# The delta rule of a two-layer sequence kernel: segment states, outputs, norm and gate on the matrix engine in a transposed layout, without a trip through memory

## Time and profile before

| | us |
|---|---|
| median of 3 runs | 1028.77 |
| lowest, highest | 1027.17, 1031.47 |
| the profiled execution | 1028.87 |
| span of its trace, first to last instruction | 1027.1 |

### The profile page before, as it was taken

How to read it: one execution, slowest core, us unless ns; L and a number is a source line. 1 busy time by engine, 2 the same in 40 slices (tenths; PEclk the granted TensorE clock), 3 DMA queues, 4 the chain that set the end, 5 groups by cost and what they waited for, 6 DMA issues and landing times.

```text
span 1027.1 us, 21006 instructions
## 1 busy us (share of the span) xinstructions
PE 652.3 (64%) x8802; PEld 463.8 (45%) x8802; DVE 690.6 (67%) x1280; ACT 383.5 (37%) x894; POOL 252.1 (25%) x179
## 2 busy tenths in 40 slices
PE   3899999999999999999987898930000000000036
PEld 2677776666776677667666364820000000000024
DVE  6377774465666566656536732389999999956987
ACT  2655555423332333233032121574454544420024
POOL 6300001000000000000010002154777777732920
PEclk9999999999999999999797799985555555555556
DMA  4100000000000000000000030000000000020001
GB/s 168 22 8 8 13 13 12 2 2 2 13 2 1 12 2 2 2 2 2 2 2 2 0 84 0 2 1 0 1 0 0 0 0 0 0 36 11 0 0 41
DMA packets 15485, 12.11 MB, mean 12 GB/s; under 512 B 8208, under 2 KB 13072, under 8 KB 15264
## 3 DMA queue, kind: packets, MB, share of 16 engines
q1 hardware_dynamic: 15392, 10.79, 4.3%
HBM read 7.21 MB, written 1.48 MB: 8 GB/s over the span
## 4 chain that ended last, share of the span: by engine, by line
PE 51%; DVE 22%; issue 14%; POOL 7%; ACT 3%; DMA 1%; SPq 1%; DVEq 0%; POOLq 0%; ACTq 0%
PE PS L550 7%; PE PS L526 7%; PE PS L425 4%; POOL arena L1001 4%; PE PS L343 3%; PE PS L331 3%; PE PS L319 3%; PE PS L542 3%; PE PS L512 3%; PE PS L673 2%; POOL arena L1007 2%; DVE arena L1169 2%; DVE arena L606 2%; PE PS L311 2%; PE PS L432 2%
## 5 line engine op out<-in xcount | busy, mean ns | idle before, releaser
L872 PE MATMUL PS<-W,arena 128*64 128x128 f32 x64 | 6.7, 403 | 311.7 <-DVE arena L1191 311.7
L606 DVE TENSOR_TENSOR arena<-PS,C 128x512 f32<-128x512 f32 x160 | 105.6, 686 | 100.8 <-PE PS L526 100.8
L872 PEld LDWEIGHTS PS<-W,arena 128*64 128x64 f32 x64 | 6.5, 226 | 311.9 <-DVE arena L1191 311.9
L927 ACT ACTIVATE arena<-arena 128x128 f32<-128x128 f32 x256 | 81.8, 390 | 99.2 <-DVE arena L1133 99.2
L526 PE MATMUL PS<-arena 64*64 64x512 f32 x640 | 89.8, 632 | 7.9 <-DVE arena L606 7.9
L990 POOL TENSOR_TENSOR arena<-arena 128x1024 f32<-128x1024 f32 x32 | 75.1, 2347 | 64.3 <-DVE arena L1133 64.3
L550 PE MATMUL PS<-arena 128*64 128x18 f32 x2560 | 89.0, 212 | 0.0
L1381 POOL TENSOR_TENSOR arena<-arena 128x512 f32<-128x512 f32 x4 | 4.9, 1264 | 341.0 <-PE PS L550 341.0
L550 PEld LDWEIGHTS PS<-arena 128*64 128x64 f32 x2560 | 85.7, 141 | 0.6
L456 ACT ACTIVATE arena<-PS 128x512 f32<-128x512 f32 (+1 forms) x48 | 23.5, 524 | 137.8 <-PE PS L427 85.5
L375 DVE TENSOR_REDUCE arena<-PS 128x4 f32<-128x512 f32 x64 | 43.9, 686 | 30.5 <-PE PS L319 30.5
(11 more groups left out here) (235 smaller groups left out, 1504.0 us busy)
## 6 DMA issues: line engine op xcount, KB each, us to landing
W<-wpack SPq DMA_DIRECT2D x1, 2532.5 KB, 10.8
arena<-arena SPq DMA_DIRECT2D x128, 16.0 KB
arena<-carry_in SPq DMA_DIRECT2D x4, 512.0 KB, 7.9
X<-x SPq DMA_DIRECT2D x4, 256.0 KB, 3.8
out<-X SPq DMA_DIRECT2D x4, 256.0 KB, 2.3
C<-cpack SPq DMA_DIRECT2D x1, 529.0 KB, 6.4
arena<-carry_out SPq DMA_DIRECT2D x4, 130.0 KB, 3.0
carry_out<-arena SPq DMA_DIRECT2D x4, 64.5 KB
```

What stands on the lines that cost most here:

```text
L606: e.tensor_tensor(AT[n % 4].rearrange("p (h t) -> p h t", h=8), PS[:, n % 2, :].rearrange("p (h t) -> p h t", h=8), tri.to_broadcast([P, 8 ...
L927: e.activation(Ra[:, cols], Rs[(t - 1) % 4][:, cols], ACT.Copy, scale=alp[:, t, h:h + 1]).then_inc(l_Ra, 1)
```

```diff
+tokt = hpack.rearrange("p (n t) -> p t n", t=CH)
+NG = CH // 4
...
+    for c in range(NQ):
+        e.matmul(PS[:, 4 + c, :], Wba.rearrange("p j c -> p (j c)"), tokt[:, quarter(c), :], start=True, stop=True)\
+         .then_inc(g_d, 1)
...
+            e.wait_ge(g_sq, i - 3)
+        for s in range(4):
+            t = 4 * i + s
...
+    for q in range(NQ):
+        if q == 3:
+            e.wait_ge(g_silu, 1)
+        e.matmul(PS[:, 5 + q % 3, :], Wgt.rearrange("p j c -> p (j c)"),
+                 hpack[:, q * SEG:(q + 1) * SEG], start=True, stop=True).then_inc(g_gate, 1)
...
+    def carry(k):
+        e.wait_ge(t_S, k + 1)
+        for b in range(NB):
+            for r in (slice(0, CH), slice(CH, P)):
+                m = e.matmul(PS[r, 7, 16 * (k % 2) + DH * b:16 * (k % 2) + DH * b + DH],
+                             Tbd[r, NC1 * b + k, :, :].rearrange("p h d -> p (h d)"), Sc[r, NC1 * b + k, :],
+                             start=True, stop=True, skip_group_check=True)
+        m.then_inc(t_P, 1)
+    def outputs(q):
+        if q == 0:
+            e.wait_ge(t_q, 2 * NQ)
+        e.wait_ge(t_Sb, q + 1)
+        for n in range(8 * q, 8 * q + 8):
+            for r in (slice(0, CH), slice(CH, P)):
+                m = e.matmul(PS[r, q, CH * (n % 8):CH * (n % 8) + CH],
+                             Sbd[r, n, :, :].rearrange("p h e -> p (h e)"), qzT[r, :, n],
+                             start=True, stop=True, skip_group_check=True)
+        m.then_inc(o_S, 1)
+    def squares(q):
+        e.wait_ge(o_sq, q + 1)
+        for i in range(4):
+            m = e.matmul(PS[:, q, i * NH:(i + 1) * NH], osq[q][:, i * P:(i + 1) * P], cst("hmask"),
...
+    def spread(q):
+        e.wait_ge(o_rt, q + 1)
+        for i in range(4):
+            m = e.matmul(PS[:, q, i * P:(i + 1) * P], osq[q][:, i * P:(i + 1) * P], ident,
+                         start=True, stop=True, skip_group_check=True)
...
+    def project(q):
+        e.wait_ge(o_n, q + 1)
         for i in range(4):
+            m = e.matmul(PS[:, 6 + q % 2, i * P:(i + 1) * P], onT[q][:, i * P:(i + 1) * P], w("L1Wo"),
...
+    for k in range(1, NC1 - 1):
+        carry(k)
+    outputs(0)
+    outputs(1)
+    outputs(2)
+    squares(0)
+    squares(1)
+    spread(0)
+    outputs(3)
+    squares(2)
+    spread(1)
+    project(0)
+    squares(3)
+    spread(2)
+    project(1)
+    spread(3)
+    project(2)
+    ln_turn(e, 3, 0)
+    project(3)
+    for q in range(1, NQ):
...
+        t4 = PS[:, i % 4, 0:4 * QW].rearrange("p (t c) -> p t c", t=4)
+        e.activation(Zs[:, 4 * i:4 * i + 4, :], t4[:, :, 0:2 * LD], ACT.Square).then_inc(g_sq, 1)
+        e.activation(pr[:, 4 * i:4 * i + 4, :], t4, ACT.Copy).then_inc(g_pr, 1)
+        if i == 1:
+            e.wait_ge(g_gd, NQ)
+            e.activation(beta, gd[:, :, 0:LH], ACT.Sigmoid).then_inc(gate_act, 1)
+            e.wait_ge(gate_dve, V_DZ)
+            e.activation(da, dz, ACT.Abs).then_inc(gate_act, 1)
+            e.activation(eA, w("Alog"), ACT.Exp).then_inc(gate_act, 1)
+            e.wait_ge(gate_act, A_ABS)
+            e.activation(da, da, ACT.Exp, scale=-1.0).then_inc(gate_act, 1)
+        if i == 3:
+            e.wait_ge(gate_dve, V_EX1)
+            e.activation(da, da, ACT.Ln).then_inc(gate_act, 1)
+        if i == 5:
+            e.wait_ge(gate_dve, V_DEC)
+            e.activation(alp, dec, ACT.Exp).then_inc(gate_act, 1)
+            e.wait_ge(gate_dve, V_GC)
+            e.activation(eg, gc, ACT.Exp).then_inc(gate_act, 1)
+        if i in (7, 9, 12):
+            root((7, 9, 12).index(i))
     root(NQ - 1)
...
+    def gates(q):
+        cols = slice(q * SEG, (q + 1) * SEG)
+        e.wait_ge(g_gate, q + 1)
+        e.activation(gt[:, cols], PS[:, 5 + q % 3, :], ACT.Silu).then_inc(g_silu, 1)
...
+        if 2 <= t < 2 + 2 * NQ:
+            (gates if t % 2 == 0 else weigh)((t - 2) // 2)
...
+    Rf = Rs[(CH - 1) % 4]
+    e.activation(Tl[:, 0:256].rearrange("p (d h i) -> p d h i", d=DH, h=LH),
+                 Rf.rearrange("p (h c d) -> p d h c", h=LH, c=2 * DH)[:, :, :, DH:2 * DH], ACT.Copy, scale=-1.0)\
...
+    def square(q):
+        e.wait_ge(o_s, q + 1)
+        e.activation(osq[q], osb[q], ACT.Square).then_inc(o_sq, 1)
+    def rms(q):
+        e.wait_ge(o_rr, q + 1)
+        e.activation(osq[q].rearrange("p (n d) -> p n d", d=DH),
+                     bc(rr[:, q, :, :].rearrange("p i (h o) -> p (i h) o", o=1), [P, 4 * NH, DH]), ACT.Sqrt).then_inc(o_rt, 1)
+    square(0)
+    square(1)
+    rms(0)
+    square(2)
+    rms(1)
+    square(3)
+    rms(2)
+    rms(3)
...
+        e.tensor_tensor(bb[:, quarter(c), :, DH:2 * DH], h4(kn)[:, quarter(c)],
+                        per_head(be[:, quarter(c), :], t=CH // NQ), ALU.mult).then_inc(g_bbk, 1)
...
+    def decayed_queries(c):
+        e.wait_ge(g_qn, c + 1)
+        e.tensor_tensor(h4(qeg)[:, quarter(c)], h4(qn)[:, quarter(c)], per_head(eg[:, quarter(c), :], t=CH // NQ), ALU.mult)\
...
+    def difference(v):
+        cols = slice(2 * v * LD, 2 * (v + 1) * LD)
+        e.wait_ge(l_z, v + 1)
+        e.wait_ge(g_qeg, v // (PAIRS // NQ) + 1)
+        e.tensor_tensor(qeg_[:, cols], qeg_[:, cols], ZK[:, cols], ALU.subtract).then_inc(l_d, 1)
...
+    for c in range(NQ):
+        e.wait_ge(g_d, c + 1)
+        e.transpose(gd[:, quarter(c), :].rearrange("p t c -> p (t c)"), PS[:, 4 + c, :]).then_inc(g_gd, 1)
+    e.wait_ge(g_gd, NQ)
+    e.tensor_tensor(dz, gd[:, :, LH:2 * LH], bc(w("dtb").rearrange("p (o h) -> p o h", o=1), [P, CH, LH]),
...
+    norms(1)
+    queries(0)
+    values(0)
+    norms(2)
+    queries(1)
+    values(1)
+    queries(2)
+    e.memset(Rs[3], 0.0).then_inc(l_R, 1)
+    norms(3)
+    values(2)
+    e.memset(rx, 0.0).then_inc(g_ready, 1)
     queries(3)
+    values(3)
...
+    def transitions(i):
+        b, n0 = i % 2, NC1 * (i % 2) + 8 * (i // 2)
+        e.wait_ge(t_tr, 2)
+        e.tensor_tensor(Tbd[:, n0:n0 + 8, :, :],
+                        bc(Tt[:, :, n0:n0 + 8].rearrange("p d (n o) -> p n o d", o=1), [P, 8, 8, DH]),
+                        bc(mask8.rearrange("p (o h x) -> p o h x", o=1, x=1), [P, 8, 8, DH]), ALU.mult).then_inc(t_bd, 1)
...
+    def states(q):
+        e.tensor_tensor(Sbd[:, 8 * q:8 * q + 8, :, :],
+                        bc(Sc[:, 8 * q:8 * q + 8, :].rearrange("p n (o e) -> p n o e", o=1), [P, 8, 8, DH]),
+                        bc(mask8.rearrange("p (o h x) -> p o h x", o=1, x=1), [P, 8, 8, DH]), ALU.mult).then_inc(t_Sb, 1)
...
+    def turn(c, dst, src):
+        e.wait_ge(l_d, (c + 1) * PAIRS // NQ)
+        cols = slice(c * 512, (c + 1) * 512)
+        e.transpose(dst[:, cols], src[:, cols]).then_inc(t_q, 1)
...
+    e.wait_ge(t_TV, 1)
+    diag = Tl.rearrange("p (d x) -> p d x", x=33)[:, :, 0:LH * DH:DH]
+    e.tensor_tensor(diag, diag, bc(eg[:, CH - 1, :].rearrange("p (o h) -> p o h", o=1), [P, DH, LH]), ALU.add)\
...
+    e.transpose(Tt.rearrange("p d n -> p (d n)"), Tl[:, 0:256]).then_inc(t_tr, 1)
...
+    e.wait_ge(t_tr, 3)
+    e.tensor_copy(Sb[:, :, 1, :], Vb[:, :, 0, :]).then_inc(t_S, 1)
+    for k in range(1, NC1 - 1):
+        e.wait_ge(t_P, k)
+        e.tensor_tensor(Sb[:, :, k + 1, :],
+                        PS[:, 7, 16 * (k % 2):16 * (k % 2) + 16].rearrange("p (b e) -> p b e", b=NB),
+                        Vb[:, :, k, :], ALU.add).then_inc(t_S, 1)
+        if k <= 2:
+            transitions(k + 1)
+        elif k <= 8 or k in (10, 11):
+            c = {3: 0, 4: 0, 5: 1, 6: 1, 7: 2, 8: 2, 10: 3, 11: 3}[k]
+            if k in (3, 5, 7, 10):
+                turn(c, qzT_, qeg_)
+            else:
+                turn(c, zvT_, ZV)
+        elif k == 9:
+            states(0)
+    states(1)
+    states(2)
+    states(3)
+    def gather(q):
+        e.wait_ge(o_S, q + 1)
+        e.wait_ge(t_q, 2 * NQ)
+        e.tensor_tensor(osb[q].rearrange("p (n t) -> p n t", n=8), PS[:, q, :].rearrange("p (n t) -> p n t", n=8),
+                        zvT[:, :, 8 * q:8 * q + 8].rearrange("p t n -> p n t"), ALU.add).then_inc(o_s, 1)
+    def mean_square(q):
+        e.wait_ge(o_ms, q + 1)
+        e.tensor_scalar(rr[:, q, :, :], PS[:, q, 0:4 * NH].rearrange("p (i h) -> p i h", i=4), 1.0 / DH, EPS_RMS,
+                        ALU.mult, ALU.add).then_inc(o_ep, 1)
+        e.wait_ge(o_ep, q + 1)
+        e.reciprocal(rr[:, q, :, :], rr[:, q, :, :]).then_inc(o_rr, 1)
+    def normalised(q):
+        e.wait_ge(o_bc, q + 1)
+        e.wait_ge(o_g, q + 1)
+        e.tensor_tensor(onT[q], ogt[q], PS[:, q, :], ALU.mult).then_inc(o_n, 1)
...
+    gather(0)
+    gather(1)
+    mean_square(0)
+    gather(2)
+    mean_square(1)
...
+    normalised(0)
+    gather(3)
+    mean_square(2)
+    normalised(1)
+    mean_square(3)
+    update(0)
+    normalised(2)
+    update(1)
+    ln_scale(e, 3, 0)
+    normalised(3)
+    e.wait_ge(h_omu, 2)
+    e.wait_ge(h_pad, 1)
+    update(2)
+    ln_scale(e, 3, 1)
+    shift(e, 0)
+    update(3)
+    ln_scale(e, 3, 2)
+    shift(e, 1)
+    ln_scale(e, 3, 3)
```

(15 more changed lines are left out.)

349 lines of the change are left out of this document (134 added, 215 removed).

## The result

Before 1029.65 us (four runs, 1027.17 to 1031.47), after 974.99 (four runs, 973.23 to 976.42): a ratio of 0.947, 95% interval 0.945 to 0.949, so 54.7 us less. Forecast were 971 (959 to 985) and faster. The profiled execution took 973.23 with a span of 970.7. But the sum came out near partly by luck: its second largest term, the 6.7 us between the stage's first matmul and the scan, was not there at all, and most of what that cost was covered by something that was not in the sum.

The account below looks back on a forecast made before the run. It took the scan as DVE's, staying at 197.9 us, and priced the stretches around it, where PE idled before and behind the scan. Sum: 1028.9 - 6.7 - 53.0 + 1.8 = 971.0 us, range 959 to 985.

Parts of the forecast that it names:

- its second largest term: Projections and gates: scan starts at 699 instead of 705.7, 6.7 us earlier, the serial part behind the projections nearly gone.
- its main case: Whole kernel: 971 us, 964 to 977, holding PE's clock at either level; chance 0.60.
- the large term: Scan's end to first residual: 36.7 us instead of 89.7, 53 us gone.
- the rival with scattered streams: Decay matmuls and outputs: scattered streams run at half rate, costing 3.4, 5.1 and 0.9 us; 980 us, chance 0.08.
- ACT lost 0.45 us for each us in which PE wrote: Projections: PE's writing to PS slows ACT's copies, 12 us of it under copies, 5.4 us lost.
- The price for ACT: Projections and gates: 26.1 us of ACT work plus 5.4 lost, 31.5 us; bounds 26.1 and 41.1.
- its list: DVE's work from the third root (about 688.5) to the scan: reciprocals, products, memset, last sum, ending at 699.
- The loads of L862 read such numbers too ... and show no cost: Projections: scattered numbers read as weights take 0.033 us apiece, cited against the rule that scattered reads are penalised.
- Carry: Behind the scan: first PE round at T + 4.5, fourteen rounds of 1.2 us each, done at T + 22.2.
- DVE's extra work: Carry rounds: a mask product or transpose, 0.7 us, hides behind PE's 0.9; otherwise 0.7 on at most 11 rounds.
- 2.4 GHz at T + 30: Behind the scan: PE's clock rises 30 us after the scan's end T, dense work having begun at T + 22.
- the two prices given: First residual behind the scan: T + 36.7 with the clock rising at T + 30, T + 41.7 at 1.2 GHz throughout.

Follow-up runs that it names:

- e1: Changed kernel with the decay matmuls reading 512 tokens side by side: scan starts 45.4 us behind the first decay matmul instead of 48.8.
- e2: Changed kernel with the projections' weight loads reading 32 tokens side by side: scan starts 40.2 us behind the first decay matmul instead of 48.8.
- f2: Kernel before the change with only hT reordered, tokens of one position side by side: 1019.41 us, ratio 0.991.
- e3: Changed kernel with POOL's last pair held until DVE made two transition products: first residual 36.9 us behind the scan instead of 37.6.
- f3: Changed kernel with the outputs' matmuls reading 64 queries side by side: three outputs 4.66 us instead of 5.57, first residual 34.0 us behind the scan.
- e9: Changed kernel with nine of POOL's key products moved into the scan: scan starts 43.9 us behind the first decay matmul instead of 48.8.
- e7: Changed kernel with idle PE matmuls around the scan's end and in each carry round: first residual 42.4 us behind the scan instead of 37.6.
- e4: Changed kernel with 64 idle PE matmuls from the last four scan steps up to the rounds: first residual 37.9 us behind the scan.

## Why the prediction was right, and where it was not

The median of 975.0 lies 4 us above the forecast of 971, inside its range and inside the 964 to 977 of its main case. The mechanism behind the large term was right, that behind the second was not, and a start that no step foresaw brought the sum back.

- **Start of the scan: wrong, 48.8 us behind the first matmul and not 42.2.** Three steps failed. The decay matmuls were priced at 0.86 us, that of an operand side by side, and took 1.72; the rival with scattered streams had this 3.4 us, at 0.08. e1 shows it. Then "ACT lost 0.45 us for each us in which PE wrote" laid on PS what came from the loads' reading (e2, f2). The price for ACT came out right all the same, 30.6 against 31.5 us, by two errors against each other: undisturbed it is 22.3 us (e2) and not 26.1, since a Square and its Copy follow every 0.63 to 0.67 us and not every 0.94, and the disturbance was 8.3 us and not 5.4. And DVE's queue decided, as said, but its list was wrong: behind the third root it begins with the third quarter's inverse, while in the code the second quarter's inverse and two products stand ahead of that, 3.1 us. From the third root to the scan it was 12.2 us and not 10.5, in the changed kernel and in e2 alike, so this part is not the loads' doing; the other 4.9 us lie ahead of the root, 3.4 of them the decay matmuls.
- **"The loads of L862 read such numbers too ... and show no cost"**: wrong. Most of their cost was in the rows of the others, in ACT's 20.09 us, read as something else. And the loads paid too: in the changed kernel they came every 0.035 us and side by side every 0.021 (e2).
- **Why the total held.** Against 971.0 the profiled execution has + 6.6 at the scan's start, + 0.9 up to the first residual, - 0.7 behind it, + 0.7 outside the span, and - 5.3 because PE's first instruction of the stage came earlier, which no step foresaw: 973.2. That is luck, as the spread of this start (651.5 to 657.6) shows. With a start as in the execution before it would have been 978.5, within the range, but outside the 964 to 977 of the main case.
- **Scan: right.** 197.9 in the changed kernel and its ten variants, also with nine more products on POOL.
- **Carry: right in kind, two sizes off.** First round at 6.4 for 4.5: the diagonal, put at 0.2, took 1.77 beside POOL (e3: 0.22 without), 1.6 of the 1.9 us. The products, 1.78 and 1.10 beside POOL, came to the 2.9 that were forecast (e3: 1.00 each without). A round took 0.88 for 1.2: PE's own part was overpriced, 0.60 for 0.93, while the add (0.18) and the two hand-overs (0.10 together) were as forecast. DVE's extra work does hide: rounds with and without a turn of 0.70 are alike at 0.88, which is also DVE's 0.18 + 0.70; with products of 1.01 a round takes 1.0.
- **Outputs: 5.57 for three, 5.1 forecast.** Scattering cost nearly nothing at 1.2 GHz (f3), so this part of the rival with scattered streams (5.1 us more) was wrong, and its first part, the decay matmuls, right.
- **Clock: late.** "2.4 GHz at T + 30" was T + 22.0 to T + 25.7 and again from T + 35.7. 37.6 lies between the two prices given, 36.7 and 41.7. Other executions had it at T + 29 to 31 and came in at 34.9 and 34.0 (e9, f3).
- **To the end: 34.9 for 35.6, right.**

So 52.1 us of the gain lie where the transfers and DVE's products of 4096 numbers were, as said (53); the 6.7 at the scan's start were not there.

## What to carry to other kernels

When several engines are slow at once, look for an instruction that is slow but shares only one thing with the suspect: here a root of 64 numbers that touches no PS. Weights that PE loads in single, distant numbers can cost the other engines more than PE; changing the order in which four copies of ACT write it cost nothing and gave 9 us even to the old kernel. And check a total term by term, stage starts against stage starts: here a term that was 6.6 us too good was covered by a start that happened to be 5.3 us early.

## What the runs showed of the hardware that was not expected

- Beside loads of 128x32 numbers 256 bytes apart, ACT's instructions took 851 ns on average instead of 385, 747 instead of 500 and 1179 instead of 501, a root in the buffer 1.26 us instead of 0.25, and one DVE turn 4.01 instead of 0.72. The loads themselves came every 0.035 us instead of every 0.021, at 2.4 GHz.
- A streamed operand of single numbers 128 or 256 bytes apart has a pace of its own: 0.86 us a record of 128x512 at 2.4 GHz for 0.43, and 0.058 a record of 64x64 at either clock for 0.056 and 0.033. A Square (0.36) and three turns (0.72) beside it kept their price.
- PE's granted clock was 1.2 GHz in the rounds of 64x8 matmuls, also in a stretch of 15 us where the records show PE busy throughout (e7), and 2.4 GHz in one of 9 us where they show it busy for 4.62 (e4).
